# Second attention: the division after the values is spread over ScalarE, VectorE and GpSimd

## What is computed

```python
# second layer: 32 heads of 16, 256 tokens, per element b
scores = jnp.einsum('bqhd,bkhd->bhqk', q, k) * scale
scores = jnp.where(causal[None, None], scores, jnp.finfo(scores.dtype).min)
probs = jax.nn.softmax(scores, axis=-1)
out = jnp.einsum('bhqk,bkhd->bqhd', probs, v).reshape(b, s, d)
return out @ wo
```

## Time and profile before

| | us |
|---|---|
| median of 3 runs | 1900.38 |
| lowest and highest | 1899.41, 1903.45 |
| the profiled execution's own time | 1903.59 |
| its span, first to last instruction | 1901.8 |

### The profile page before, as it was taken

How to read it: one execution, slowest core, us unless ns; L and a number is a source line. 1 busy time by engine, 2 the same in 40 slices (tenths; PEclk the granted TensorE clock), 3 DMA queues, 4 the chain that set the end, 5 groups by cost and what they waited for, 6 DMA issues and landing times.

```text
span 1901.8 us, 38226 instructions
## 1 busy us (share of the span) xinstructions
PE 1845.8 (97%) x12792; PEld 1542.3 (81%) x12792; DVE 1507.3 (79%) x2398; ACT 885.1 (47%) x2246; POOL 864.8 (45%) x870
## 2 busy tenths in 40 slices
PE   8999979999999999999999999999999989999997
PEld 5788968888888888888888888887898856666786
DVE  4677678788888888888888888788889658889887
ACT  3333334444444444444444444456555356667343
POOL 0133364444444444444444444354576646666011
PEclk9999989999999999999999999999999989999999
DMA  9677741111111111111111111222387776554121
GB/s 360 204 245 243 250 137 50 51 50 50 46 43 45 50 50 50 50 44 42 46 50 50 50 50 42 90 94 70 115 241 225 232 229 188 163 165 120 39 67 61
DMA packets 202713, 211.41 MB, mean 111 GB/s; under 512 B 19178, under 2 KB 172778, under 8 KB 201868
## 3 DMA queue, kind: packets, MB, share of 16 engines
q1 hardware_dynamic: 201124, 208.49, 35.5%
q10 hardware_dynamic: 1512, 1.90, 0.3%
HBM read 128.40 MB, written 73.53 MB: 106 GB/s over the span
## 4 chain that ended last, share of the span: by engine, by line
PE 69%; issue 12%; DVE 8%; SPq 4%; POOL 4%; DMA 2%; ACT 1%; DVEq 0%; POOLq 0%; ACTq 0%
PE ps L1140 18%; PE ps L1101 17%; PE ps L1114 7%; PE ps L1129 5%; PE ps L1152 4%; SPq L1413 3%; PE ps L1124 3%; POOL k_rot L637 2%; PE ps L2688 2%; PE ps L2724 2%; DVE f_neg_max L2101 2%; PE ps L2282 1%; PE ps L2309 1%; PE ps L2313 1%; PE ps L2236 1%
## 5 line engine op out<-in xcount | busy, mean ns | idle before, releaser
L1140 PE MATMUL ps<-wo,ot 128*128 (+1 forms) x1536 | 380.4, 396 | 0.0
L1140 PEld LDWEIGHTS ps<-wo,ot 128*128 128x128 f32 x1536 | 280.4, 189 | 54.7
L888 ACT ACTIVATE prob<-ps,neg_max 128x128 f32<-128x128 f32 (+1 forms) x512 | 208.2, 419 | 132.8 <-DVE neg_max L975 110.6
L1101 PE MATMUL ps<-ht_hi,wq 128*128 (+1 forms) x1024 | 253.2, 389 | 1.3 <-DVE q_swap L940 0.9
L1054 POOL TENSOR_TENSOR q_rot<-q_rot,q_swap 128x512 f32<-128x512 f32 x128 | 166.9, 1304 | 178.6 <-DVE q_swap L940 178.6
L895 ACT ACTIVATE pt<-ps 128x512 fp32r<-128x512 f32 x192 | 108.0, 598 | 274.6 <-PE ps L1152 274.5
L1101 PEld LDWEIGHTS ps<-ht_hi,wq 128*128 128x128 f32 x1024 | 192.0, 188 | 41.8 <-issue 1.3
L1048 POOL TENSOR_TENSOR prob<-prob,inv_sum 128x512 f32<-128x512 f32 x64 | 66.6, 1041 | 273.7 <-DVE inv_sum L984 273.7
L1114 PE MATMUL ps<-pt,vv 128*128 128x512 f32 x576 | 144.0, 394 | 4.5 <-issue 3.9
L955 DVE TENSOR_TENSOR ot<-ps,ot 128x512 fp32r<-128x512 f32 x128 | 88.3, 691 | 74.5 <-ACT ot L905 74.5
L2101 DVE TENSOR_REDUCE f_neg_max<-ps 128x4 f32<-128x512 f32 (+1 forms) x128 | 116.8, 953 | 33.5 <-PE ps L2227 26.3
(11 more groups left out here) (255 smaller groups left out, 4053.4 us busy)
## 6 DMA issues: line engine op xcount, KB each, us to landing
stack_dram<-e_part SPq DMA_DIRECT2D x192, 128.0 KB, 2.4
v_dram<-v_part SPq DMA_DIRECT2D x32, 512.0 KB, 5.9
k_dram<-k_part SPq DMA_DIRECT2D x64, 256.0 KB, 2.6
kk<-k_dram SPq DMA_DIRECT2D x128, 128.0 KB, 2.1
vv<-v_dram SPq DMA_DIRECT2D x128, 128.0 KB, 2.1
f_q<-stack_dram SPq DMA_DIRECT2D x124, 104.0 KB
f_k<-stack_dram SPq DMA_DIRECT2D x124, 104.0 KB
wmod<-in_wmod SPq DMA_DIRECT2D x12, 1024.0 KB, 14.6
```

The source lines that it names most:

```text
L888: nc.scalar.activation(p[:, h], sc[:, h], ACT.Exp, bias=neg_max[:, t, h:h + 1], accum_out=row_sum[:, t, h:h + 1]).then_inc(p_exp, 1)
L1101: mm = nc.tensor.matmul(ps_q[j][:], w[:, at:at + HD0], r[:, bass.ds(b, 2), k], start=(n == 0), stop=(n == len(passes) - 1))
L1140: mm = nc.tensor.matmul(ps_y[j][:], o[:, j, h * P:(h + 1) * P], w[:, bass.ds(at + h * D, D)], start=(n == 0), stop=(n == len(passes) - 1))
```

## The change

The division of one half t of a pair was done on VectorE alone. Now ScalarE copies the undivided output half from PSUM to a new SBUF tile `f_kept` (`kept`), VectorE takes the reciprocal only, and GpSimd multiplies the two SBUF tiles (`divided`) and reports `o_out`. There is one new semaphore, `o_kept`, which VectorE's reciprocal awaits. The copy of half 1 waits for the reciprocal of half 0 (`o_rcp`); both read the same PSUM bank.

```diff
@@ VectorE
         def output(w, i, t):
             cols = slice(t * P, (t + 1) * P)
-            dve.wait_ge(o_done, 2 * w + 2)
+            dve.wait_ge(o_kept, 2 * w + t + 1)
             nc.vector.reciprocal(inv_sum[i][:, cols], ps_o[i][:, 1, cols]).then_inc(o_rcp, 1)
-            dve.wait_ge(o_rcp, 2 * w + t + 1)
-            dst = keep.ot1_raw[:, bass.ds(w, 1), cols].rearrange("p o s -> p (o s)")
-            nc.vector.tensor_tensor(dst, ps_o[i][:, 0, cols], inv_sum[i][:, cols], ALU.mult).then_inc(o_out, 1)
@@ ScalarE
+        def kept(w, i, t):
+
+            act.wait_ge(o_done, 2 * w + 2)
+            act.wait_ge(o_out, 2 * w + t + 3)
+            if t:
+                act.wait_ge(o_rcp, 2 * w + 1)
+            nc.scalar.activation(kept_out[t][:], ps_o[i][:, 0, t * P:(t + 1) * P], ACT.Identity).then_inc(o_kept, 1)
+
         def step(v, slot, at):
+            if 3 <= at and slot % 2:
+                kept((v - 3) // 2, (slot + 1) // 2 % 2, 0)
+            if 4 <= at and not slot % 2:
+                kept((v - 4) // 2, slot // 2, 1)
             if 0 <= at < U - 1:
                 negated(act, v + 1, (slot + 1) % NS)
             if 0 <= at < U:
...
         steps(act, step)
+        for t in range(TT):
+            kept(PAIRS - 1, 1, t)
         high(PAIRS - 2)
         high(PAIRS - 1)
@@ GpSimd
+        def divided(w, t, i):
+
+            cols = slice(t * P, (t + 1) * P)
+            pool.wait_ge(o_rcp, 2 * w + t + 1)
+            dst = keep.ot1_raw[:, bass.ds(w, 1), cols].rearrange("p o s -> p (o s)")
+            nc.gpsimd.tensor_tensor(dst, kept_out[t][:], inv_sum[i][:, cols], ALU.mult).then_inc(o_out, 1)
...
+                if at >= 4:
+                    pool.wait_ge(o_out, v + 1)
                 if at >= 6 and slot % 2:
                     pool.wait_ge(o_split, (v - 5) // 2)
                 negated_again(v + 1, (slot + 1) % NS)
                 pool.wait_ge(m_again, v + 2)
             if 0 <= at < U:
                 cut(v, slot)
+            if 3 <= at and slot % 2:
+                divided((v - 3) // 2, 0, (slot + 1) // 2 % 2)
+            if 4 <= at and not slot % 2:
+                divided((v - 4) // 2, 1, slot // 2)
             if 6 <= at and not slot % 2:
                 low((v - 6) // 2)
```

More of the change, by code:

```diff
@@ L2031, in attention1 @@
     neg_max = [over(f"f_neg_max{s}", [P, TT, HU]) for s in range(2)]
+    kept_out = [over(f"f_kept{t}", [P, P]) for t in range(TT)]
     ps_o = [keep.ps[:, 6 + i].rearrange("p (n s) -> p n s", n=2) for i in range(2)]
@@ L2050, in attention1 @@
     o_done = sem("f_o_done")
+    o_kept = sem("f_o_kept")
     o_rcp = sem("f_o_rcp")
@@ L2220, in gpsimd @@
         steps(pool, step)
+        for t in range(TT):
+            divided(PAIRS - 1, t, 1)
         low(PAIRS - 2)
```

## The result

The changed kernel takes 1907.47 us, the median of 7 runs (1906.13 to 1911.10); seven runs of the kernel before, the three told above among them, have the median 1902.36 (1899.41 to 1903.48). The ratio is 1.0032, with a 95% interval from 1.0021 to 1.0043: slower by 0.3%, or some 6 us. The profiled execution after took 1908.87 us with a span of 1907.0, against 1903.59 and 1901.8 before.

What follows compares the result with a forecast made beforehand. PE was taken as the bound, busy 119.13 of 122.09 us in the loop. Terms 11.5 + 0.5 - 1.7 - 1.1 + 0.3 + 0.3 = +9.8 on the median 1900.38 gave 1910 us, range 1905 to 1916 (eight in ten).

Steps and rivals of the forecast that it cites:

- the single row: PE's second mask waiting for the copy of the maxima (L2140): seen once, 0.4 us; slack otherwise 0.19 us.
- my bounds (308 and 366): Length of ScalarE's new copy in ns: plain 128x128 copy from SBUF below, exponential from PSUM above; 0.31 us taken.
- the prediction's two circles: Two loops closing in a 3.34 us step: PE's own work, and early scores through VectorE's reductions to the next L2261.
- even steps 16 to 60: Half 1's copy awaits half 0's reciprocal, delaying the maxima's copy and PE's second mask: 23 x 0.50 = +11.5 us.
- steps 6 to 14: Five more even steps with the copy's delay, where PE also waits for DMA operands: +0.5 us, from 0 to 2.5.
- first steps of a round: VectorE passes the loop's branch beside the reciprocal, so nine waits for the reductions go, about 0.19 each: -1.7 us.
- steps 56 to 61: Without the product VectorE needs 3.23 us instead of 3.52, so PE is the bound again: 6 x 0.18 = -1.1 us.
- product beside the subtraction: GpSimd's product comes behind VectorE's subtraction L2577, late for three beginning pairs: 3 x 0.1 = +0.3 us (0 to 0.9).
- the end: Last pair's half 1 copy and `high` wait longer, with some slack before L2721: +0.3 us, from -0.2 to +0.5.
- the second rival: GpSimd's product takes 0.8 to 1.4 us and L2309 waits at pair beginnings: up to +14, on average 1919; chance 0.08.
- the rival that the first copy also delays the maxima: Half 0's copy delays L2140 by 0.2 us more in 23 odd steps: +4.6, 1915 us; chance 0.12.
- VectorE's relief is worth more than the circles show: Rival: PE idles 3.0 us in 122; with all of it won, and the end, 1896 us; chance 0.03.

Runs made afterwards that it cites:

- first experiment: Changed kernel with the even step's ScalarE copy of half 1 moved behind the copy of the maxima; 1900.58 us, ratio 0.9986 to the kernel before.
- second experiment: Changed kernel with one more, useless 128x128 ScalarE copy between the even step's copy and the maxima; 1911.39 us, ratio 1.0040 to the kernel before.
- the fourth experiment: Changed kernel without the repeated wait for `o_done` ahead of the copy of half 1; one time 1909.41 us, 161.42 us from step 16 to 62.
- the sixth experiment: Changed kernel with half 1's copy behind the maxima's copy and PE's early scores ahead of the near turned scores; 1899.83 us, ratio 0.9976 to before.
- the third: Kernel before without the ones matmuls for the second 128 keys on PE; one time 1900.99 us, 156.58 us from step 16 to 62.

## Why the prediction was right, and where its size was off

**The mechanism.** The prediction named the instruction that would be late (the copy of the maxima), what it would wait behind (the copy of half 1, for half 0's reciprocal), the slack that this would use up and the steps that would get longer. The traces show each of these, and the first two experiments show that it is the cause: taking the delay away turns +5.14 into -2.38, adding 0.20 to it adds 0.20 to each even step. What decided was the single row: a wait that is hardly ever seen, with 0.19 us of slack under it.

**The number.** The forecast was 1910 us, the result 1907.47, but only half of the forecast change came: +9.8 was forecast, +5.1 is the difference of the medians (+6.1 by the ratio). The absolute number comes nearer because the median of before, 1900.38 of three runs, rose to 1902.36 with four more; that is luck. The lower bound of 1905 was under what the prediction's own terms gave at their least (+7.8, so 1908.2), and that margin was needed.

**The step that was mis-sized: "Behind it on PE are the late scores, the values and the next L2261, all back to back, so the whole step moves."** The term was 23 x 0.50 = +11.5; measured is 9 x 0.30 + 14 x 0.38 = +8.0. Two things make the difference.

- The delay of the mask itself was well sized. It starts 1.64 us into a first step (1646.34 - 1644.70) against 1.23 before (1648.66 - 1647.43), 0.41 late. The copy took 278 ns, less than either of my bounds (308 and 366), and L2139 starts 0.18 us after it: its register instruction costs nothing beside the copy. In mid-round it is some 0.08 more, with the waits of the fourth experiment.
- But the step grew by 0.30, not by 0.41. From the start of L2337 to the next L2289 it is 1.44 us (1646.90 to 1648.34) where it was 1.55 before (1649.22 to 1650.77). PE had 0.11 in hand at the end of the step, because the next L2261 waited for the reductions, and the prediction's two circles were not equally long: the sixth experiment, where PE never idles, has the same 1.44, and the third shows which circle bound. The prediction had seen both, and then costed the delay as if PE's own were the only one. The other circle got longer nearly as much: with the mask late, the second reduction waits for the late scores (0.18) and ends at 1648.27, 0.07 ahead of the next L2289, where before it was 0.06. So in the changed kernel too the two limits lie within some 0.02 us.

| term | forecast, us | measured, us |
|---|---|---|
| even steps 16 to 60 | +11.5 | +8.0 |
| steps 6 to 14 | +0.5 (0 to 2.5) | not told apart from the loads |
| first steps of a round | -1.7 | -1.7, but only beside the copy's delay |
| steps 56 to 61 | -1.1 | -1.1 |
| product beside the subtraction | +0.3 | 0 |
| the end | +0.3 | +0.2 |
| sum | +9.8 | 8.0 - 1.7 - 1.1 = +5.2 by steps, +5.14 in the trace |

The measured rows count every step from a base of 3.34, as the forecast did, so their sum is right. Their names are not: with the copy alone, and the product still on VectorE, the loop's steps are the same as in after. Of the two minus terms only 3 x 0.16 us (the odd steps from 57 on) come from VectorE's relief then. In the other steps the mask's wait has taken the place of the wait for the reductions, and the difference of the two is what the step shows.

**Steps 6 to 14.** The waits of after between 1553 and 1602 us still have the loads, three in place of four:

```profile
PEld ps L2255 <- DMA f_k<-stack_dram: 3.1, 3, 1.6
```

Steps 6 and 12, which lie between loads, are 3.64 and 3.72 in place of 3.34. Whether a later load takes this up no run shows: the start of step 16 spreads by 7.6 us over the runs, so that a half microsecond can't be read there.

**GpSimd's product.** Its rows in the trace of after, by form (count; busy us, mean ns; idle time before), the loop's first, then the written-out steps', and VectorE's subtraction:

```profile
L2217 POOL TENSOR_TENSOR turned_raw<-f_kept,f_inv_sum 128x128 f32 x48 | 22.0, 459 | 20.4 <-DVE f_inv_sum L2109 20.4
L2217 POOL TENSOR_TENSOR turned_raw<-f_kept,f_inv_sum 128x128 f32<-128x128 f32 x16 | 10.5, 657 | 11.7 <-DVE f_inv_sum L2109 11.7
L2605 DVE TENSOR_TENSOR g_lo<-g_raw,g_w 128x512 fp32r<-128x512 f32 x8 | 6.4, 803 | 0.0
```

In the loop it is 459 ns where 0.47 was forecast. In no step do PE's values wait for it (the only one that ever does is `high`, at the end), so the second rival falls. The term +0.3 failed by its sizes. The values that need the product stand in odd steps, such as step 57, which begins at 1739.74 (timeline of after):

```profile
1740.45 0.63 DVE L2605 TENSOR_TENSOR g_lo<-g_raw,g_w 128x512 fp32r<-128x512 f32 x1
1740.62 0.78 POOL L2217 TENSOR_TENSOR turned_raw<-f_kept,f_inv_sum 128x128 f32<-128x128 f32 x1 [0.67 <-DVE f_inv_sum L2109]
...
1741.55 0.64 PE L2337 MATMUL ps<-f_prob,f_v 128*32 128x256 f32 x8
```

The subtraction starts earlier than I had taken it, 0.71 us into the step, and takes 0.63; the stretched product ends at 1.66 us, where 1.9 was forecast and the values start at 1.81. In even steps, where no values wait for a product, the subtraction takes 0.71 to 1.02 us and the product 0.85 to 0.90; the 803 ns are the mean of these kinds, before it was 683.

**The half-0 copy, and VectorE's relief.** Odd steps are 3.34 to 3.35, so the rival that the first copy also delays the maxima falls. That VectorE's relief is worth more than the circles show falls as well: where the copy is out of the way the steps give 2.38 us (forecast 1.7 + 1.1), and no step of the loop falls under 3.34.

**The end.** From the start of half 0's last reciprocal to the start of L2749 (L2721 before) it is 8.14 us, against 7.93 before: +0.2. The timeline of after shows the way over GpSimd's product (0.96 us there) with `high` (L2155) waiting for it:

```profile
1772.55 0.95 DVE L2109 RECIPROCAL f_inv_sum<-ps 128x128 f32<-128x128 f32 x1
1773.61 0.28 ACT L2163 ACTIVATE f_kept<-ps 128x128 f32<-128x128 f32 x1 [2.05 <-DVE f_inv_sum L2109]
1773.92 0.96 DVE L2109 RECIPROCAL f_inv_sum<-ps 128x128 f32<-128x128 f32 x1 [0.43 <-ACT f_kept L2163]
1774.96 0.96 POOL L2217 TENSOR_TENSOR turned_raw<-f_kept,f_inv_sum 128x128 f32<-128x128 f32 x1 [0.92 <-DVE f_inv_sum L2109]
1775.96 0.42 ACT L2155 ACTIVATE turned<-turned_raw 128x256 fp32r<-128x256 f32 x1 [1.76 <-POOL turned_raw L2217]
...
1780.69 0.47 PE L2749 MATMUL ps<-g_bias,g_row_r 128*128 128x512 f32 x1 [0.22 <-DVE g_hs L2619]
```

## What to carry to other kernels

Before an instruction with a wait is put into an engine that works in order, ask what stands behind it and how much slack that has, also where the profile shows no wait: here a wait seen once in 1900 us had 0.19 us of cover, and one instruction's place was worth 7.5 us. When a delay is then costed, subtract at every place downstream what the next engine was waiting for anyway, and don't add gains and losses that fall in the same step: the later of the two limits counts alone. A TensorE that is 97% busy can still be paced by another engine; shortening its work in an experiment shows which circle binds.

## What the runs showed of the hardware

The contention between VectorE and GpSimd works **in both directions**. I had used it in one: a GpSimd instruction is held up by VectorE's subtraction of two SBUF tiles. The first experiment's rows show the other: the subtraction starts at 1735.22 while GpSimd's `cut` runs until 1734.47 + 1.22 = 1735.69, and ends 0.55 us after that, at 1736.24. The product that starts at 1735.66 lasts until 1736.55, so these intervals fit a subtraction that was held until the cut had ended and a product held behind the subtraction. The Trainium skill (SBUF — State Buffer, Who interferes with whom) has this: whichever of the two engines issues first keeps the access that they share, and the other waits. The trace agrees, with 1.02 us against 0.68 for the same subtraction.

The timelines of all nine kernels bear it out step by step. Wherever a GpSimd instruction (a cut, in some cases a cast) still ran 0.13 us or more after the start of this subtraction, the subtraction lasted 0.54 us beyond its end: 0.70 us in all when that was after 0.16, 0.80 after 0.26, 0.91 after 0.37, 1.02 after 0.48. And the product that started while the subtraction ran ended some 0.3 us after it, whether that had taken 0.63 or 1.02.

A 128x128 copy from PSUM on ScalarE took 277 ns on average of the 64 in after, one from SBUF 302 ns (the median of the 31 added in the second experiment). The instruction behind the copy started 0.18 us after its start (1645.54 to 1645.72), with a register instruction between.
